# First adapter number read from DRAM, first weight chunk in two halves of k, ScalarE copies of the float32 chunks, a base block's sum later

## The chip, the cores and the metric

The kernel runs on one core of a Trainium2 chip. A core has TensorE (PE, matmuls), VectorE (DVE), ScalarE (ACT), GpSimd (POOL) and SyncE (SP), each with its own instruction queue, and 16 DMA engines that all queues share. The metric is the device time of one execution in microseconds (us), lower is better.

## The reference

For each of 8 batch elements, x is 256 tokens by 1024. A weight of 1024x1024 is picked by the element's adapter number, and the product goes through a feed-forward layer with a router over 15 entries that map to 8 experts of rank 16:

```python
w = weight[adapter_ids]
y = jnp.einsum('bsi,boi->bso', x, w)
base_out = jnp.einsum('btd,od->bto', y, base_W) + base_b
logits = jnp.einsum('btd,nd->btn', y, router_W) + router_b
probs = jax.nn.softmax(logits, axis=-1)
topk_p, topk_i = jax.lax.top_k(probs, E)
mapped = expert_map[topk_i]
onehot = (mapped[..., None] == jnp.arange(E)).astype(y.dtype)
w = jnp.einsum('btk,btke->bte', topk_p, onehot)
h = jnp.einsum('btd,erd->bter', y, A)
lora = jnp.einsum('bter,eor->bto', h * w[..., None], B) * 2.0
out = x + base_out + lora
```

All data is float32. The adapter numbers (`ids`) are an input in DRAM.

## The kernel before

Each element has two stages. **Stage 1** makes y in 8 chunks (`OC`) of 128 output columns, one weight chunk of 512 KB each, contracted over 8 blocks of k (`KC`). **Stage 2** multiplies y by the base weight, the router and the experts. To reach float32 accuracy at the rate of the fp32r type, every operand is split: ACT rounds it to fp32r (the `_hi` tile), DVE subtracts (`_lo`), and PE multiplies hi by hi, hi by lo and lo by hi. For element 0 alone the first two chunks (`F32_CHUNKS = 2`) are plain float32 matmuls on the raw weights (`stage1_float32`, L841 to L850), so that nothing has to be split ahead of them. Before them PE runs 13 warm-up matmuls (L962).

The base weight is used as seven blocks (Strassen-like): four loaded (r00, r01, r10, r11) and sums of them. `block_sum_1` (L703 to L706) makes r01 - r00 on DVE into the place of T1; ACT then rounds it (L483) and DVE makes its lo part (`t1_lo`, L722). `block_hi` (L431) and `block_lo` (L686) do the same for a loaded block: B00, B10 and B11 are numbers 1, 2 and 3 on the semaphore `blocks_lo_done`.

The order of the work is written by hand, one queue for each engine:

- SP loads the adapter numbers to SBUF (`ids_sb`, L269), waits for them, reads number 0 into a register (`adapter`, L272), issues the load of weight chunk 0 with it (L335, semaphore `w0_in`), then chunks 1 to 3 (L275), chunks 4 to 7 into early buffers (L339), the stage 2 weights, and later the residual and element 1.
- ACT issues the two halves of x of element 0 (`load_x0`, L373), rounds them (L460), rounds weight chunks 2 and 3 (`adapter_hi`) and 4 and 5 (`early_hi`), and goes through its loop over chunks (L465 to L479): `evacuate` copies the second half of a chunk's PSUM bank out, `make_y_hi` rounds a pair of chunks of y, and at chunk 6 it rounds block B00.
- DVE makes the lo parts of x (L768) and of the weights (L509, L514); in its loop over chunks (L771 to L786) it copies the two float32 chunks out of PSUM (L774), adds the halves of the others (`make_y_sum`, L527), makes y_lo of each pair (`make_y_lo`, L531), and at chunk 6 runs `block_sum_1`. Behind the loop come B00's and B10's lo parts, masks, routing, the two adds of the first products (`p1_added`), t1_lo, gates, B11's and b's lo parts, bias, `make_hwt_lo`, bias, x of element 1, `block_sum_2`, two weight chunks of element 1, `block_sum_4`, and the final adds (L787 to L822); then element 1 (L739).
- PE runs chunks 0 to 7, then `first_stage2` (L896 to L921), then elements 1 to 7. A chunk c waits for its weight's lo part and for `y_sum_done` of chunk c - 2 (L833, L834), since two PSUM banks alternate.

`make_y_lo` of a pair (j, j+4) is waited for by `plain` (L859): the last pair (3, 7) is used last, at PE's 13th k-step of it. `product(w_ps, ..., B10)` waits for `p1_added` 1 and `product(x_ps, ..., B10)` for `p1_added` 2 (L904, L906).

Of the kernel before, what the change touches and what calls it, by code (L numbers as in the profile page):

```python
# [36 lines left out]
def adaln_ffn_kernel(nc, xT, x, ids, wT, a_t, base_t, b_t, router_t, base_b, router_b, expert_map, out):  # L37
# [28 lines left out]
    with ExitStack() as ctx:  # L66
        def sem(name):
            return ctx.enter_context(nc.semaphore(name))
# [92 lines left out]

        ids_in = sem("ids_in")
        x0_in = [sem(f"x0_in{j}") for j in range(PIECES)]
        w0_in = sem("w0_in")
        x_in = [sem(f"x_in{h}") for h in range(2)]
        w_in = [sem(f"w_in{s}") for s in range(W_SLOTS)]
        early_in = [sem(f"early_in{i}") for i in range(OC - W_SLOTS)]
# [98 lines left out]

        @block.sync
        def _(sp):
            sp.dma_start(ids_sb[:, :], ids).then_inc(ids_in, 16)  # L269

            def adapter(b):
                return sp.value_load(ids_sb[0:1, bass.ds(b, 1)], min_val=0, max_val=wT.shape[0] - 1)  # L272

# [17 lines left out]
            def load_res(b, t, first=False):  # L291
                if not first:
                    if isinstance(b, int) and b == 1:
                        sp.wait_ge(stored_first[t], 16)
                    else:
                        sp.wait_ge(stored[t], 16 * (b - 1))
                sp.dma_start(res[:, t, :], x[b, t * P:(t + 1) * P, :] if first else
                             x[bass.ds(b, 1), t * P:(t + 1) * P, :].rearrange("b p d -> (b p) d")).then_inc(res_in[t], 16)
# [31 lines left out]
                        load_w(nxt, c)  # L330
                store_element(b, last)

            sp.wait_ge(ids_in, 16)
            id0 = adapter(0)
            sp.dma_start(w_raw[:, 0, :, :], wT[bass.ds(id0, 1), 0].rearrange("a p k o -> (a p) k o")).then_inc(w0_in, 16)  # L335
            for c in range(1, W_SLOTS):
                load_w(id0, c)
            for i in range(OC - W_SLOTS):
                sp.dma_start(early_raw[i][:, :, :], wT[bass.ds(id0, 1), ORDER[W_SLOTS + i]].rearrange("a p k o -> (a p) k o")).then_inc(early_in[i], 16)  # L339
            sp.dma_start(a_raw[:, :, :], a_t).then_inc(ar_in, 16)  # L340
            sp.dma_start(router_raw[:, :, :], router_t).then_inc(ar_in, 16)
            for h in range(2):
# [10 lines left out]
            sp.wait_ge(x0_lo_done, PIECES)  # L353
            for t in range(NT):
                load_res(0, t, first=True)
            id1 = adapter(1)
            for c in range(W_SLOTS):
                sp.wait_ge(y_ps_done, W_SLOTS + c + 1)
# [11 lines left out]
        def _(act):  # L370
# [12 lines left out]
            def adapter_hi(b, c):  # L383
                act.wait_ge(w_in[c % W_SLOTS], 16 * w_uses(b, c))
                nc.scalar.copy(w_hi[:, c % W_SLOTS, :, :], w_raw[:, c % W_SLOTS, :, :]).then_inc(w_hi_done, 1)  # L385

            def early_hi(c):

                act.wait_ge(early_in[c - W_SLOTS], 16)
                if c - W_SLOTS >= F32_CHUNKS:  # L390
                    act.wait_ge(y_ps_done, c - W_SLOTS + 1)
                nc.scalar.copy(w_hi[:, c % W_SLOTS, :, :], early_raw[c - W_SLOTS][:, :, :]).then_inc(w_hi_done, 1)
# [64 lines left out]
            for j in range(PIECES):  # L457
                k = slice(j * KP, (j + 1) * KP)
                act.wait_ge(x0_in[j], 16)
                nc.scalar.copy(x_split[:, k, 0, :], x0_raw[:, k, :]).then_inc(x0_hi_done, 1)  # L460
            for c in (2, 3):
                adapter_hi(0, c)
            for c in (4, 5):
                early_hi(c)
            for c in range(OC):  # L465
                if c >= F32_CHUNKS:
                    evacuate(0, c)
# [37 lines left out]
        def _(dve):  # L505
# [180 lines left out]
            def block_lo(n, block_of, src):  # L686

                dve.wait_ge(blocks_hi_done, n)
                nc.vector.tensor_tensor(st_lo[:, :, block_of, :], src, st_hi[:, :, block_of, :], ALU.subtract).then_inc(blocks_lo_done, 1)
# [13 lines left out]
            def block_sum_1():  # L703
                dve.wait_ge(r00_in, 16)
                dve.wait_ge(r01_in, 16)
                nc.vector.tensor_tensor(r_t1, r01, r00, ALU.subtract).then_inc(t_done, 1)  # L706
# [62 lines left out]
            for c in (2, 3):  # L769
                adapter_lo(0, c)  # L770
            for c in range(OC):  # L771
                if c < F32_CHUNKS:
                    dve.wait_ge(y_ps_done, c + 1)
                    nc.vector.tensor_copy(y_sum[:, ORDER[c], :], y_ps[:, c, 0:T]).then_inc(y_sum_done, 1)  # L774
                else:
                    make_y_sum(0, c)
                if c % 2:
                    make_y_lo(0, c // 2)
                if c < OC - W_SLOTS:
                    early_lo(c + W_SLOTS)  # L780
                if c == 4:
                    ar_lo()
                if c in (5, 6):
                    plain_lo(c - 5)
                if c == 6:
                    block_sum_1()  # L786
            block_lo(1, B00, r00)  # L787
            block_lo(2, B10, r10)
            masks()
            routing_logits(0)  # L790
# [39 lines left out]
        def _(pe):  # L830
# [10 lines left out]
            def stage1_float32(c):  # L841
                if c > 0:
                    pe.wait_ge(w_in[c], 16)
                for k in range(KC):
                    if c == 0 and k == 0:
                        pe.wait_ge(w0_in, 16)
                    if c == 0 and k % KP == 0:
                        pe.wait_ge(x0_in[k // KP], 16)
                    mm = nc.tensor.matmul(y_ps[:, c, 0:T], w_raw[:, c, k, :], x0_raw[:, k, :], start=(k == 0), stop=(k == KC - 1))  # L849
                mm.then_inc(y_ps_done, 1)  # L850
# [174 lines left out]
```

## Time and profile before

| | us |
|---|---|
| median of 3 runs | 403.43 (403.35 to 403.43) |
| profiled execution, its time | 404.47 |
| span of the profiled execution, first to last instruction | 402.7 |
| PE busy / DVE busy / ACT busy | 395.6 / 306.3 / 157.0 |

The span is what the profile's rows cover; 1.8 us of the profiled execution lie around it. Times in rows are microseconds from the span's start. PE is TensorE's matmuls, PEld its weight loads; "q1" is the DMA queue of SP, "q10" that of ACT, "q0" that of GpSimd. "idle before <-releaser" is how long the engine stood still ahead of the instruction, and what let it go.

### The profile page before, as it was taken

What the parts mean: (1) busy time and instruction counts of PE and PEld (TensorE: products, weight loads), DVE (VectorE), ACT (ScalarE), POOL (GpSimd) and SP (SyncE); (2) the same over time, 40 slices, a digit from 0 to 9 for tenths busy, and PEclk for the clock granted to TensorE, in tenths of its full rate; (3) what the DMA queues carried; (4) which work ended last, traced back from release to release, by engine and by line L of the source; (5) the groups of instructions that cost most, each with busy time, mean ns of one, the idle gap of its engine ahead of it and who ended that gap; (6) DMA issues with size and microseconds to landing.
All of it is one profiled execution on the core that took longest, in us unless ns stands there. A gap on an engine that the chain in (4) does not pass through costs nothing.

```text
span 402.7 us, 5975 instructions
## 1 busy us (share of the span) xinstructions
PE 395.6 (98%) x2102; PEld 348.9 (87%) x2102; DVE 306.3 (76%) x564; ACT 157.0 (39%) x223; POOL 2.0 (0%) x10
## 2 busy tenths in 40 slices
PE   6999999999999999999999999999999999999996
PEld 6888888888888888889888888888888898888885
DVE  2669999879978985688748896589856899468763
ACT  3658342663136421564025530265304642144300
POOL 0000001000000000000000000000000000000000
PEclk9999999999999999999999999999999999999999
DMA  7999106840268305573066520775026830464002
GB/s 287 396 392 399 48 0 208 278 144 0 104 221 300 105 0 174 190 260 104 0 208 226 213 81 0 260 256 200 13 68 245 292 125 0 138 225 161 2 0 104
DMA packets 25693, 64.71 MB, mean 161 GB/s; under 512 B 3410, under 2 KB 12626, under 8 KB 25682
## 3 DMA queue, kind: packets, MB, share of 16 engines
q1 hardware_dynamic: 25106, 62.47, 43.6%
q10 hardware_dynamic: 288, 1.05, 0.8%
q0 software_dynamic: 288, 1.05, 0.7%
q8 instruction: 6, 0.10, 0.1%
q14 instruction: 5, 0.04, 0.0%
HBM read 56.18 MB, written 8.39 MB: 160 GB/s over the span
## 4 chain that ended last, share of the span: by engine, by line
PE 86%; DVE 8%; ACT 2%; DMA 2%; issue 1%; SPq 0%; DVEq 0%
PE y_ps L836 26%; PE y_ps L838 13%; PE pl_ps L861 6%; PE x_ps L872 6%; PE x_ps L871 6%; PE x_ps L873 6%; PE s_ps L871 5%; PE s_ps L872 5%; PE s_ps L873 5%; PE pl_ps L862 3%; PE y_ps L849 2%; DMA w_raw<-in_wT 1%; DVE w_lo L509 1%; DVE res L618 1%; PE s_ps L886 1%; PE s_ps L888 1%
## 5 line engine op out<-in xcount | busy, mean ns | idle before, releaser
L836 PE MATMUL y_ps<-x_split,w_hi 128*128 128x512 f32 x496 | 173.4, 393 | 0.5 <-DVE y_sum L527 0.5
L838 PE MATMUL y_ps<-x_split,w_lo 128*128 128x256 f32 x496 | 138.9, 280 | 0.0
L836 PEld LDWEIGHTS y_ps<-x_split,w_hi 128*128 128x128 f32 x496 | 92.8, 187 | 22.0 <-DVE w_lo L509 1.1
L838 PEld LDWEIGHTS y_ps<-x_split,w_lo 128*128 128x128 f32 x496 | 93.7, 189 | 0.4
L385 ACT CAST w_hi<-w_raw 128x1024 fp32r<-128x1024 f32 x58 | 60.8, 1050 | 77.2 <-DMA w_raw<-in_wT 77.1
L509 DVE TENSOR_TENSOR w_lo<-w_raw,w_hi 128x1024 fp32r<-128x1024 f32 x58 | 70.9, 1224 | 19.5 <-ACT w_hi L385 17.9
L377 ACT COPY y_sum<-y_ps 128x256 f32<-128x256 f32 x62 | 23.0, 371 | 59.6 <-PE y_ps L838 59.6
L861 PE MATMUL pl_ps<-pl_split,y_hi 128*128 128x480 f32 x128 | 42.7, 383 | 0.0
L618 DVE TENSOR_TENSOR res<-x_ps,res 128x464 f32<-128x464 f32 (+1 forms) x30 | 19.5, 651 | 27.2 <-PE x_ps L888 15.1
L527 DVE TENSOR_TENSOR y_sum<-y_ps,y_sum 128x256 f32<-128x256 f32 x62 | 26.0, 420 | 15.2 <-ACT y_sum L377 15.0
L862 PE MATMUL pl_ps<-pl_split,y_lo 128*128 128x240 f32 x128 | 34.9, 273 | 0.0
L871 PE MATMUL s_ps<-st_hi,y_hi 128*128 128x464 f32 x80 | 30.5, 381 | 0.1
L618 DVE TENSOR_TENSOR res<-s_ps,res 128x512 f32<-128x512 f32 (+1 forms) x32 | 20.9, 675 | 11.9 <-PE s_ps L888 11.9
L872 PE MATMUL s_ps<-st_lo,y_hi 128*128 128x464 f32 x80 | 29.9, 373 | 0.0
L873 PE MATMUL s_ps<-st_hi,y_lo 128*128 128x464 f32 x80 | 29.7, 372 | 0.0
L381 ACT CAST y_hi<-y_sum 128x512 fp32r<-128x512 f32 x32 | 19.8, 620 | 23.7 <-DVE y_sum L527 23.1
L861 PEld LDWEIGHTS pl_ps<-pl_split,y_hi 128*128 128x128 f32 x128 | 24.1, 188 | 4.0
L531 DVE TENSOR_TENSOR y_lo<-y_sum,y_hi 128x512 fp32r<-128x512 f32 x32 | 22.1, 692 | 5.5 <-ACT y_hi L381 2.7
L862 PEld LDWEIGHTS pl_ps<-pl_split,y_lo 128*128 128x128 f32 x128 | 24.3, 190 | 0.0
L872 PE MATMUL x_ps<-st_lo,y_hi 128*128 128x464 f32 x64 | 23.9, 373 | 0.0
L871 PE MATMUL x_ps<-st_hi,y_hi 128*128 128x464 f32 x64 | 23.8, 373 | 0.0
L873 PE MATMUL x_ps<-st_hi,y_lo 128*128 128x464 f32 x64 | 23.8, 371 | 0.0
(111 smaller groups left out, 536.2 us busy)
## 6 DMA issues: line engine op xcount, KB each, us to landing
w_raw<-in_wT SPq DMA_DIRECT2D x60, 512.0 KB, 3.6
res<-in_x SPq DMA_DIRECT2D x16, 512.0 KB, 4.7
x_raw<-in_xT SPq DMA_DIRECT2D x14, 512.0 KB, 4.8
out<-res SPq DMA_DIRECT2D x13, 512.0 KB, 3.1
early_raw<-in_wT SPq DMA_DIRECT2D x4, 512.0 KB, 9.1
hi_raw<-in_base_t SPq DMA_DIRECT2D x2, 928.0 KB, 9.7
st_raw<-in_base_t SPq DMA_DIRECT2D x2, 928.0 KB, 10.8
x_raw<-in_xT ACTq DMA_DIRECT2D x2, 512.0 KB, 4.4
```

The costliest lines, as they stand in the source:

```text
L377: nc.scalar.copy(y_sum[:, ORDER[c], :], y_ps[:, c % 2, T:2 * T]).then_inc(y_part_done, 1)
L385: nc.scalar.copy(w_hi[:, c % W_SLOTS, :, :], w_raw[:, c % W_SLOTS, :, :]).then_inc(w_hi_done, 1)
L509: nc.vector.tensor_tensor(w_lo[:, s, :, :], w_raw[:, s, :, :], w_hi[:, s, :, :], ALU.subtract).then_inc(w_lo_done, 1)
L527: nc.vector.tensor_tensor(y_sum[:, o, :], y_ps[:, c % 2, 0:T], y_sum[:, o, :], ALU.add).then_inc(y_sum_done, 1)
L618: return nc.vector.tensor_tensor(res[:, t, cols], ps, res[:, t, cols], ALU.add)
L836: nc.tensor.matmul(y_ps[:, c % 2, :], w_hi[:, s, k, :], x_split[:, k, :, :].rearrange("p s t -> p (s t)"), start=(k == 0), stop=False)
L838: mm = nc.tensor.matmul(y_ps[:, c % 2, 0:T], w_lo[:, s, k, :], x_split[:, k, 0, :], start=False, stop=(k == KC - 1))
L861: nc.tensor.matmul(pl_ps[:, t, 0:2 * PL], hi, pl_split[:, k, :, :].rearrange("p s n -> p (s n)"), start=(k == 0), stop=False)
L862: mm = nc.tensor.matmul(pl_ps[:, t, 0:PL], lo, pl_split[:, k, 0, :], start=False, stop=(k == KC - 1))
L871: nc.tensor.matmul(dst, hi(j), st_hi[:, j, block_of, :], start=begins and j == 0, stop=False, skip_group_check=not begins)
L872: nc.tensor.matmul(dst, hi(j), st_lo[:, j, block_of, :], start=False, stop=False, skip_group_check=not begins)
L873: mm = nc.tensor.matmul(dst, lo(j), st_hi[:, j, block_of, :], start=False, stop=(j == KH - 1), skip_group_check=not begins)
```

## The change

Four edits, all in the work of element 0. SP reads adapter number 0 straight from DRAM into its register, and the DMA that brings the numbers to SBUF, for the later elements, moves behind the weight loads. The load of weight chunk 0 is split by k into two DMAs of 256 KB with a semaphore each, and chunk 0's matmuls wait for them one half at a time. The copies of the two float32 chunks out of PSUM move from DVE to ACT, between the roundings of weight chunks 2 to 5. On DVE, the lo part of block B00 moves from behind the chunk loop to chunk 6, where `block_sum_1` was, and `block_sum_1` moves behind the loop, ahead of B10's lo part.

```diff
-        w0_in = sem("w0_in")
+        w0_in = [sem(f"w0_in{j}") for j in range(PIECES)]
...
-            sp.dma_start(ids_sb[:, :], ids).then_inc(ids_in, 16)
-
...
-            sp.wait_ge(ids_in, 16)
-            id0 = adapter(0)
-            sp.dma_start(w_raw[:, 0, :, :], wT[bass.ds(id0, 1), 0].rearrange("a p k o -> (a p) k o")).then_inc(w0_in, 16)
+            id0 = sp.value_load(ids[0:1, 0:1], min_val=0, max_val=wT.shape[0] - 1)
+            for j in range(PIECES):
+                k = slice(j * KP, (j + 1) * KP)
+                sp.dma_start(w_raw[:, 0, k, :], wT[bass.ds(id0, 1), 0, :, k].rearrange("a p k o -> (a p) k o")).then_inc(w0_in[j], 16)
             for c in range(1, W_SLOTS):
                 load_w(id0, c)
             for i in range(OC - W_SLOTS):
...
+            sp.dma_start(ids_sb[:, :], ids).then_inc(ids_in, 16)
             sp.dma_start(a_raw[:, :, :], a_t).then_inc(ar_in, 16)
...
+            sp.wait_ge(ids_in, 16)
             id1 = adapter(1)
...
-            for c in (2, 3):
-                adapter_hi(0, c)
-            for c in (4, 5):
-                early_hi(c)
+            def evacuate_float32(c):
+                act.wait_ge(y_ps_done, c + 1)
+                nc.scalar.copy(y_sum[:, ORDER[c], :], y_ps[:, c, 0:T]).then_inc(y_sum_done, 1)
+
+            adapter_hi(0, 2)
+            evacuate_float32(0)
+            adapter_hi(0, 3)
+            early_hi(4)
+            evacuate_float32(1)
+            early_hi(5)
...
             for c in range(OC):
-                if c < F32_CHUNKS:
-                    dve.wait_ge(y_ps_done, c + 1)
-                    nc.vector.tensor_copy(y_sum[:, ORDER[c], :], y_ps[:, c, 0:T]).then_inc(y_sum_done, 1)
-                else:
+                if c >= F32_CHUNKS:
                     make_y_sum(0, c)
...
                 if c == 6:
-                    block_sum_1()
-            block_lo(1, B00, r00)
+                    block_lo(1, B00, r00)
+            block_sum_1()
             block_lo(2, B10, r10)
...
-                    if c == 0 and k == 0:
-                        pe.wait_ge(w0_in, 16)
                     if c == 0 and k % KP == 0:
+                        pe.wait_ge(w0_in[k // KP], 16)
                         pe.wait_ge(x0_in[k // KP], 16)
```

## Rows read from the trace of the kernel before

**Rows 1.** The page's 40 slices of the span: the granted clock in tenths.

```profile
PEclk9999999999999999999999999999999999999999
```

**Rows 2.** Waits of PE over the whole span: us in total, times, longest.

```profile
PE y_ps L849 <- DMA w_raw<-in_wT: 1.7, 1, 1.7
```

**Rows 3.** The chain of waits, first 8.5 us: start, us, what.

```profile
0.73 1.19 DMA ids_sb<-in_ids
1.94 0.46 SPq L272
2.89 5.57 DMA w_raw<-in_wT
```

**Rows 4.** Timeline of PE, 0 to 16 us.

```profile
1.50 5.33 PE L962 MATMUL s_ps<-ident 128*128 128x128 f32 x26 [1.50 <-POOL ident L978]
8.50 7.17 PE L849 MATMUL y_ps<-x_raw,w_raw 128*128 128x256 f32 x32 [1.67 <-DMA w_raw<-in_wT]
```

**Rows 5.** Line L272, all its instructions, then the one of 0 to 3 us.

```profile
L272 SPq TENSOR_LOAD <-ids_sb x15: 268/499/673, 1.9 to 352.6; - x15
...
L272 SPq TENSOR_LOAD <-ids_sb x1: 462/462/462, 1.9 to 1.9; - x1
```

**Rows 6.** DMA queues in 4.4 to 4.9 us, then in 4.9 to 5.4 us.

```profile
q10 hardware_dynamic: 51, 0.21, 101.5%
...
q1 hardware_dynamic: 18, 0.07, 75.2%
```

**Rows 7.** SP's timeline at 63.75, then DMA queues in 65.00-65.45, 65.45-65.90 us.

```profile
63.75 5.96 SPq L275 DMA_DIRECT2D w_raw<-in_wT  x3
...
q0 software_dynamic: 19, 0.08, 78.5%
...
q1 hardware_dynamic: 17, 0.07, 37.5%
```

**Rows 8.** Timeline of ACT, 4 to 14 us: start, us, engine, line.

```profile
4.59 1.04 ACT L460 CAST x_split<-x_raw 128x1024 fp32r<-128x1024 f32 x1 [1.69 <-DMA x_raw<-in_xT]
6.16 1.05 ACT L460 CAST x_split<-x_raw 128x1024 fp32r<-128x1024 f32 x1 [0.53 <-DMA x_raw<-in_xT]
11.00 1.04 ACT L385 CAST w_hi<-w_raw 128x1024 fp32r<-128x1024 f32 x1 [3.79 <-DMA w_raw<-in_wT]
12.27 1.04 ACT L385 CAST w_hi<-w_raw 128x1024 fp32r<-128x1024 f32 x1 [0.23 <-DMA w_raw<-in_wT]
```

**Rows 9.** Timeline of DVE, and one row of ACT at 30.27, 30 to 39 us.

```profile
30.27 1.75 ACT L432 CAST st_hi<-hi_raw 128x1856 fp32r<-128x1856 f32 x1
...
30.88 2.08 DVE L706 TENSOR_TENSOR hi_raw<-hi_raw 128x1856 f32<-128x1856 f32 x1
32.88 0.41 DVE L527 TENSOR_TENSOR y_sum<-y_ps,y_sum 128x256 f32<-128x256 f32 x1
33.98 0.69 DVE L531 TENSOR_TENSOR y_lo<-y_sum,y_hi 128x512 fp32r<-128x512 f32 x1 [0.69 <-ACT y_hi L381]
...
38.59 0.17 DVE L693 CAST map_f<-map_i 128x15 f32<-128x15 int32 x1
```

**Rows 10.** Timeline of PE at 36.12 and 42.49, and of DVE at 41.03.

```profile
36.12 0.38 PE L861 MATMUL pl_ps<-pl_split,y_hi 128*128 128x480 f32 x1
...
42.49 0.37 PE L871 MATMUL s_ps<-st_hi,y_hi 128*128 128x464 f32 x1
...
41.03 0.63 DVE L618 TENSOR_TENSOR res<-s_ps,res 128x464 f32<-128x464 f32 x1
```

**Rows 11.** Timeline of DVE, 50 to 70 us.

```profile
50.87 0.42 DVE L610 TENSOR_TENSOR hwt_lo<-s_ps,hwt_hi 128x256 fp32r<-128x256 f32 x1 [0.46 <-ACT hwt_hi L419]
...
64.35 1.22 DVE L509 TENSOR_TENSOR w_lo<-w_raw,w_hi 128x1024 fp32r<-128x1024 f32 x1 [0.20 <-DVE res L618]
...
68.96 0.42 DVE L527 TENSOR_TENSOR y_sum<-y_ps,y_sum 128x256 f32<-128x256 f32 x1
```

**Rows 12.** Timeline of PE, 69 to 73 us: chunks 3 and 4 of element 1.

```profile
69.52 0.47 PE L836 MATMUL y_ps<-x_split,w_hi 128*128 128x512 f32 x1 [0.34 <-DVE y_sum L527]
...
72.72 0.47 PE L836 MATMUL y_ps<-x_split,w_hi 128*128 128x512 f32 x1 [0.18 <-DVE y_sum L527]
```

## The prediction

> **What bounds the kernel now.** I read the page first: PE is busy 395.6 of 402.7 us and the granted clock is full in every slice [rows 1], so only time in which PE stands still can be won. The waits of PE come next: the one large wait behind the warm-up is 1.7 us for weight chunk 0 [rows 2]. The timeline of PE places it: the warm-up ends at 6.83, and chunk 0 begins at 8.50 [rows 4]. The chain of waits names what ends it: the adapter numbers' DMA (0.73 to 1.92), the register load (1.94 to 2.40), and the weight's DMA, issued at 2.89 and landed at 8.46 [rows 3]. Later PE stands still twice more, before chunks 3 and 4 of element 1, at 69.52 and 72.72, and both times DVE is the releaser [rows 12]. The timeline of DVE shows why: from 50.87 to 64.35 it works without a gap over 0.2 us, then through two weight chunks up to the y_sum of 68.96, on which chunk 3 waits [rows 11]. So the kernel has two tight places: its start, bound by a DMA, and 51 to 73 us, bound by DVE. What is won at the start must pass the second place to reach the end.
>
> Call X the time by which chunk 0 begins earlier. It can't exceed 8.50 - 6.83 = 1.67 us, since the warm-up stands ahead of it [rows 4].
>
> **Register load from DRAM.** Removed: the 1.19 us DMA and the wait for it. The SBUF load of 0.46 us becomes a DRAM load, a thing the trace doesn't have. Lower end: the fastest SBUF load, 0.27 us [rows 5]. Upper end: it takes as long as what it replaces, from 0.73 to 2.40, that is 1.67 us, since that also fetches the number from DRAM and then reads it; longer can't be excluded. I take the middle between this load's 0.46 from SBUF and 1.67, about 1.07 us, for the fetch is one trip to DRAM without descriptors. The register work between load and issue stays, 2.89 - 2.40 = 0.49 us. The first issue then falls at 0.73 + 1.07 + 0.49 = 2.29, which is 0.60 us earlier; the ends give 1.40 us earlier and none.
>
> The Trainium skill (Runtime: NRT & Kernel Launch, The ~15µs preamble/postamble breakdown) puts a load of a few registers from HBM at about 1.3 us, and a note on the same page has some 200 ns a register. By 1.3 us, an estimate from that page, the issue would be 0.37 us earlier and the total 0.2 us worse than my sum. No row here shows such a load.
>
> **Does an earlier issue make the data earlier?** The x halves are ahead of the weight. SP's queue moves no weight in 4.4 to 4.9 us, while ACT's queue fills the engines (101.5%); 18 packets of SP's queue start in 4.9 to 5.4, the first some 2.0 us behind the issue at 2.89 [rows 3, 6]. Either the engines serve x until it is through (then an earlier issue wins nothing), or a queue that joins a busy one needs about 2 us. The other place with two queues speaks for the second: SP's load issued at 63.75 has no packet until 65.45 and 17 in the 0.45 us after, while GpSimd's store is far from through and keeps moving [rows 7]; that is 1.7 us with no need to let the other finish. I take it that the start moves with the issue; sharing with the rest of x takes about 0.1 us of the 0.60 back, so 0.50. Ends: 0 and 1.3.
>
> **Two halves.** Weight chunks land one behind another every 12.27 - 11.00 = 1.27 us [rows 8], so half a chunk lands 0.63 us before the whole. The second half is needed 7.17 / 4 = 1.8 us behind PE's start, a half of a chunk [rows 4], so it is hidden, and so is the one more issue (about 0.4 us on SP's queue): chunk 2 lands at 11.00 and PE needs its split at 15.3. The Trainium skill (DMA: Bandwidth & Descriptors, Rules for kernel authors) says of two transfers to partition halves "Don't bother — they serialize". That is no loss here, because serial is what is wanted: the two x halves, issued together, were taken up at 4.59 and 6.16 [rows 8]. If instead both halves finished together, the 0.63 would be gone.
>
> X is then 0.50 + 0.63 = 1.13 us, and PE begins at 7.37. With the ends X is between 0.63 (less, if the register load takes over 1.67 us) and the cap of 1.67.
>
> **ScalarE's copies.** ACT does two copies of about 0.4 us instead of DVE. They lie in ACT's idle time (3.79 us before 11.00) or move early_hi(5), whose chunk PE needs 8 us later. PE's chunk 2 needs y_sum of chunk 0: ACT gives it behind w_hi of chunk 2, 11.00 + 1.04 + 0.4 = 12.4, well before the 15.3 - 1.1 = 14.2 at which PE comes. DVE's copy came only at 14.49 and would have held PE for about 0.7 us, so this edit is needed for X to survive; it is worth nothing by itself, for DVE has gaps up to chunk 7 and follows PE there.
>
> **Block sum later.** Here the order on DVE at the last chunk matters. I give times in PE's frame, as if X were 0, and subtract X at the end. Before: the sum r01 - r00 started at 30.88 without waiting for anything, y_sum of chunk 7 at 32.88, y_lo at 33.98 [rows 9]. After: B00's lo part must wait for ACT's rounding, 30.27 + 1.75 = 32.02 [rows 9]; it runs 32.05 to 34.05, so y_sum of chunk 7 begins at 34.05 and y_lo at 34.05 + (33.98 - 32.88) = 35.15. DVE is 1.17 us late; the rest of its queue is the same work (the sum and B00's lo part have changed places, both 2.0 us), so masks start at 38.59 + 1.17 = 39.76. Who waits?
> PE needs y_lo of the last pair at 36.12 [rows 10]; it is done at 35.15 + 0.69 = 35.84, hidden by 0.3 us.
> PE's product at 42.49 needs the add of 41.03 [rows 10]. The add now ends at 41.03 + 1.17 + 0.63 = 42.83, and PE resumes some 0.14 us after DVE's end (68.96 + 0.42 = 69.38, and PE at 69.52 [rows 11, 12]), so at 42.97: a new stall of 0.48 us. The next pair is covered by it.
> At 50.87 DVE had stood still for 0.46 us for ACT's hwt_hi [rows 11]. That gap now takes up part of the lateness: DVE reaches hwt_lo at 50.41 + 1.17 = 51.58, and ACT's part is ready at 51.3, so DVE is late by 51.58 - 50.87 = 0.71, say 0.7 us.
> From there DVE has no gap, so chunk 3 of element 1, which waits for DVE's y_sum of 68.96, comes at 69.52 + 0.7 in PE's frame, and chunk 4 at 72.72 + 0.7. The 0.48 us stall is inside this, not on top. Behind chunk 4 every wait is on work that follows PE, so the shift stays.
>
> **Sum.** The end moves by X - 0.7 = 1.13 - 0.7 = 0.43 us. Span 402.7 - 0.4 = 402.3 us, profiled execution 404.47 - 0.4 = 404.0, and the median, which is 1.04 us below the profiled execution, 403.43 - 0.4 = 403.0 us.
>
> **The rivals.**
> A, the start gains, the middle takes it all: the weight's packets can't start before x is through (rows 6 read the first way). X is 0.63 and the end comes 0.07 us later: 403.5 us. For it: x is issued 1.2 to 1.8 us ahead of the weight and fills the engines. Against: rows 7.
> B, the register load is quick (up to 0.5 us) and PE begins straight behind the warm-up: X 1.67, gain 0.97: 402.5 us. For it: SBUF loads of 0.27 [rows 5].
> C, the other side: the register load from DRAM waits behind x's traffic and takes about 2.6 us. The issue is then at 0.73 + 2.6 + 0.49 = 3.82, 0.93 us later; X = 0.63 - 0.93 = -0.3, and with the 0.7 us of the later block sum 404.4 us. It decides from X under 0.7, that is from a load over about 1.6 us; over 0.2% slower needs over 2.5 us.
> D, DVE's lateness is no bound: if something between 51 and 69 us waits for PE after all, the 0.7 doesn't arise and X comes through whole: 403.43 - 1.13 = 402.3 us. Against it: the row of 64.35 has a gap of 0.20 on DVE's own work [rows 11].
>
> **How the numbers follow.** 0.2% is 0.8 us, about what a measurement of this kernel can tell from no change. Forecast 0.45, A 0.2, B 0.15, C 0.08, D 0.12. Faster by over 0.8 us: half of B to all of it and most of D, together 0.22. Slower by over 0.8: most of C, 0.06. Within: 0.72. The range goes from B with a bit (402.4) to A with a register load near 2 us (403.43 + 0.7 - 0.3 = 403.8, and 0.1 for spread, 403.9).
>
> **What would show each step.** The first weight issue on SP near 2.3; the first packets of SP's queue near 4.3; chunk 0 on PE at about 7.4, with its second half unwaited; no PE gap before chunk 2; DVE's y_lo of the last pair about 1.2 us later against PE; a PE gap of about 0.5 us at the B10 product; gaps before chunks 3 and 4 of element 1 together about 0.7 us more than before. Wrong would be a later first issue, or an unchanged gap at chunk 3 with an early start.

## The result: 0.18% slower, and a profile of after that is shorter than that of before

The changed kernel takes 404.31 us (median of 13, 403.76 to 404.82) against 403.49 us for the kernel before, timed beside it (403.15 to 403.88): ratio 1.0018, 95% interval 1.0010 to 1.0026. I had forecast 403.0, and a range up to 403.9. The profiled execution of after took 404.08 us with a span of 402.3 us; the one of before took 404.47 and 402.7. So the two profiles say 0.4 us faster where the medians say 0.8 us slower. That is the first thing to explain: the profiled execution of before lies above all 13 timed ones. That the profile of after comes so close to the forecast for it (404.08 against 404.0) is luck, as the steps below show: two terms of the sum were wrong, and 0.2 us of the 0.4 arose behind the start of element 1, where nothing was changed.

The page of after, busy shares and the granted clock (full in every slice, as in [rows 1]):

```profile
PE 396.0 (98%) x2102; PEld 348.3 (87%) x2102; DVE 305.6 (76%) x562; ACT 157.7 (39%) x225; POOL 2.0 (0%) x10
...
PEclk9999999999999999999999999999999999999999
```

The waits of PE in after (us in total, times, longest). The wait for the weight is 0.4 us instead of the 1.7 of [rows 2]; new is the one for DVE's add (L625), at the B10 product:

```profile
PE s_ps L965 <- POOL ident L981: 1.5, 1, 1.5
PE y_ps L840 <- DVE y_sum L534: 0.6, 2, 0.4
PE y_ps L852 <- DMA w_raw<-in_wT: 0.4, 1, 0.4
PE s_ps L874 <- DVE res L625: 0.3, 1, 0.3
```

The chain of waits in after, first 11 us (start, us, what), which answers to [rows 3]. The register load from DRAM is two loads, 0.86 us for the pointer to the tensor and 2.11 us for the number itself (the rows of line L331 stand below); the first weight issue comes at 4.20, not at 2.29 as I had it and not at 2.89 as before. The chain then goes through the load of chunk 1, issued at 5.33 and landed at 10.75, for which PE stands:

```profile
0.71 0.86 SPq L331
1.59 2.11 SPq L331
3.74 0.17 SPq L331
4.20 0.40 SPq L334
4.79 0.35 SPq L334
5.33 5.42 DMA w_raw<-in_wT
10.79 0.48 PE y_ps L852
```

```profile
L331 SPq TENSOR_LOAD <-in_ids_ptr x1: 857/857/857, 0.7 to 0.7; - x1
L331 SPq TENSOR_LOAD <-in_ids x1: 2109/2109/2109, 1.6 to 1.6; - x1
```

And yet PE starts early. The timeline of PE in after, against [rows 4] and [rows 10]: chunk 0 at 6.94, the B10 product at 42.22 with a gap. Below them are four rows of DVE: B00's lo part, which waits 1.09 us for ACT's rounding, y_lo of the last pair, the add that the B10 product waits for, and hwt_lo, ahead of which DVE no longer stands still (0.46 us in [rows 11]):

```profile
6.94 7.58 PE L852 MATMUL y_ps<-x_raw,w_raw 128*128 128x256 f32 x32 [0.37 <-DMA w_raw<-in_wT]
...
42.22 0.45 PE L874 MATMUL s_ps<-st_hi,y_hi 128*128 128x464 f32 x1 [0.27 <-DVE res L625]
...
31.29 2.09 DVE L696 TENSOR_TENSOR st_lo<-hi_raw,st_hi 128x1856 fp32r<-128x1856 f32 x1 [1.09 <-ACT st_hi L433]
...
34.40 0.69 DVE L538 TENSOR_TENSOR y_lo<-y_sum,y_hi 128x512 fp32r<-128x512 f32 x1 [0.69 <-ACT y_hi L382]
...
41.45 0.63 DVE L625 TENSOR_TENSOR res<-s_ps,res 128x464 f32<-128x464 f32 x1
...
50.74 0.42 DVE L617 TENSOR_TENSOR hwt_lo<-s_ps,hwt_hi 128x256 fp32r<-128x256 f32 x1
```

Chunks 3 and 4 of element 1, against [rows 12]:

```profile
69.39 0.47 PE L840 MATMUL y_ps<-x_split,w_hi 128*128 128x512 f32 x1 [0.38 <-DVE y_sum L534]
72.58 0.47 PE L840 MATMUL y_ps<-x_split,w_hi 128*128 128x512 f32 x1 [0.18 <-DVE y_sum L534]
```

### The profile page after: what moved, and what is told of

It is laid out like the page before. It is cut to its first block, busy times and chain, and to the rows that moved or that the text cites. A ratio compares the mean times of both kernels' runs of the same rounds, so it can differ in the third digit from the quotient of the medians.

```text
span 402.3 us, 5980 instructions
## 1 busy us (share of the span) xinstructions
PE 396.0 (98%) x2102; PEld 348.3 (87%) x2102; DVE 305.6 (76%) x562; ACT 157.7 (39%) x225; POOL 2.0 (0%) x10
## 4 chain that ended last, share of the span: by engine, by line
PE 80%; DVE 13%; ACT 3%; DMA 1%; issue 1%; SPq 1%; DVEq 0%
PE y_ps L840 26%; PE y_ps L842 13%; PE pl_ps L864 5%; PE x_ps L875 5%; PE x_ps L874 5%; PE x_ps L876 5%; PE s_ps L874 4%; PE s_ps L875 4%; PE s_ps L876 4%; PE pl_ps L865 3%; DVE st_lo L696 2%; DVE res L625 1%; DMA w_raw<-in_wT 1%; DVE w_lo L516 1%; PE s_ps L889 1%
## 5 line engine op out<-in xcount | busy, mean ns | idle before, releaser
L625 DVE TENSOR_TENSOR res<-x_ps,res 128x464 f32<-128x464 f32 (+1 forms) x30 | 19.5, 651 | 27.5 <-PE x_ps L891 15.1
L534 DVE TENSOR_TENSOR y_sum<-y_ps,y_sum 128x256 f32<-128x256 f32 x62 | 26.1, 420 | 15.4 <-ACT y_sum L378 15.2
L625 DVE TENSOR_TENSOR res<-s_ps,res 128x512 f32<-128x512 f32 (+1 forms) x32 | 20.9, 675 | 11.9 <-PE s_ps L891 11.9
L382 ACT CAST y_hi<-y_sum 128x512 fp32r<-128x512 f32 x32 | 19.9, 621 | 23.4 <-DVE y_sum L534 23.4
L538 DVE TENSOR_TENSOR y_lo<-y_sum,y_hi 128x512 fp32r<-128x512 f32 x32 | 22.2, 692 | 5.4 <-ACT y_hi L382 2.6
```

Source lines behind the costliest of these rows:

```text
L534: nc.vector.tensor_tensor(y_sum[:, o, :], y_ps[:, c % 2, 0:T], y_sum[:, o, :], ALU.add).then_inc(y_sum_done, 1)
L625: return nc.vector.tensor_tensor(res[:, t, cols], ps, res[:, t, cols], ALU.add)
```

## The experiments

"before" in a time is always the kernel before, timed beside the run on the same chip. Chips and hours differ (its medians were 403.5 to 404.5 us), so only ratios are compared between groups. For each trace I read five landmarks from the timeline of PE; they carry most of what follows:

| trace | chunk 0 | stage 2 of el. 0 | element 1 | element 2 | element 3 | span |
|---|---|---|---|---|---|---|
| before | 8.50 | 32.16 | 60.55 | 110.40 | 158.78 | 402.7 |
| b_again (before) | 7.51 | 31.47 | 59.88 | 109.59 | 157.74 | 401.6 |
| before_3 (before) | 7.21 | 31.71 | 60.09 | 109.81 | 158.21 | 402.1 |
| after | 6.94 | 31.45 | 60.38 | 110.12 | 158.40 | 402.3 |
| after_again | 6.87 | 31.46 | 60.37 | 110.12 | 158.55 | 402.4 |
| after_3 | 6.81 | 31.43 | 60.33 | 110.26 | 158.78 | 402.6 |
| a_sbuf_ids | 7.21 | 31.18 | 60.10 | 109.88 | 159.16 | 403.0 |
| a_sum_early | 6.92 | 31.41 | 59.81 | 109.87 | 158.17 | 402.0 |
| a_whole_w0 | 7.48 | 31.45 | 60.34 | 110.76 | 160.12 | 404.0 |
| b_sum_late | 7.60 | 31.55 | 60.47 | 110.21 | 158.51 | 402.4 |
| b_dram_ids | 7.19 | 31.80 | 60.19 | 109.87 | 158.06 | 401.9 |
| b_halves_act | 7.24 | 31.24 | 59.65 | 109.47 | 157.75 | 401.6 |
| halves_act_2 (the same) | 7.21 | 30.84 | 59.23 | 109.10 | 157.66 | 401.5 |
| halves_act_3 (the same) | 7.44 | 31.40 | 59.80 | 109.68 | 158.11 | 402.0 |
| halves_only | 7.26 | 31.75 | 60.15 | 110.02 | 158.54 | 402.4 |
| act_only | 7.43 | 31.08 | 59.47 | 109.34 | 158.69 | 402.6 |
| sum_behind | 7.43 | 31.09 | 60.78 | 110.70 | 159.16 | 403.0 |
| x1_late | 6.19 | 30.96 | 59.35 | 109.22 | 157.78 | 401.7 |
| pool_sum2 | 7.31 | 30.96 | 61.96 | 112.18 | 160.41 | 404.3 |
| after_pool | 6.96 | 31.70 | 66.22 | 115.11 | 163.62 | 407.5 |

Where I give a stall of PE as a row's idle time, its start comes 0.16 us later still, since matmuls otherwise overlap their predecessors by that much.

Two things outside the edits move these landmarks. The 26 warm-up matmuls end anywhere from 6.09 to 7.42 us, and in three traces (after_3, halves_act_2, x1_late) the weight has landed 0.14 to 0.41 us before chunk 0 begins, so that there the warm-up sets its start. And PE's pace differs, which the next section shows; it is worth 0.3 us up to stage 2. What sets either isn't known.

From element 3 to the last matmul every trace takes 240.6 us. What is won or lost is decided before 160 us.

### How steady is the kernel before: b_again and before_3

No edit.

> The kernel before once more, for a second trace of it. Theory 1 (what the edits do to waits explains the loss): times within 0.1% of the kernel before, and a trace in which PE stands still at the same three places as in the first (about 0.5, 0.35 and 0.3 us at 69.5, 72.7 and 102.5). Theory 2 (PE's pace differs from execution to execution: a pair of an L836 and an L838 matmul took 347 ns in most stretches of the trace of before and 353 ns in 60 to 85 and 120 to 132 us): this trace is shorter than the first, about 401.7 us, with more pairs at 347 ns.

> The kernel before, third trace. If its usual start is the second trace's, weight chunk 0 lands at 7.4 to 7.7 and PE begins at 7.5; if both kinds are common, 8.5 is as likely. Element 1 begins at 59.9 in the first case, 60.5 in the second.

b_again: 403.67 us, before 403.67, ratio 1.0002 (0.9993 to 1.0011), profiled execution 403.43. before_3: 404.09, before 404.19, ratio 0.9994 (0.9978 to 1.0010). In b_again the chain of waits has the same steps as [rows 3], issued at 2.88, but the weight's DMA takes 4.59 us and not 5.57:

```profile
0.72 1.18 DMA ids_sb<-in_ids
1.92 0.46 SPq L272
...
2.88 4.59 DMA w_raw<-in_wT
7.51 1.56 PE y_ps L849 x6
```

So the same kernel starts PE at 8.50, 7.51 or 7.21 us, and the trace I predicted from had the latest start of the three. In before_3, where the start was earliest, PE then stood ahead of chunk 2 for DVE's copy of chunk 0, which came at 14.42, at its usual place:

```profile
14.99 0.47 PE L836 MATMUL y_ps<-x_split,w_hi 128*128 128x512 f32 x1 [0.60 <-DVE y_sum L774]
...
14.42 0.42 DVE L774 COPY y_sum<-y_ps 128x256 f32<-128x256 f32 x1
```

Theory 2, the pace, holds in part. A pair of an L836 and an L838 matmul takes 347 or 353 ns, in long stretches, in the same program. The timeline of PE at 20 us, before and then b_again, shows the next pair 0.34 and 0.35 us on; over the pairs of 15.4 to 31 us the means are 347 and 353 ns. Of the 20 traces nine have the first and eleven the second there. It is worth 0.3 us in 48 pairs:

```profile
20.03 0.39 PE L836 MATMUL y_ps<-x_split,w_hi 128*128 128x512 f32 x1
...
20.37 0.39 PE L836 MATMUL y_ps<-x_split,w_hi 128*128 128x512 f32 x1
```

```profile
20.17 0.40 PE L836 MATMUL y_ps<-x_split,w_hi 128*128 128x512 f32 x1
...
20.52 0.40 PE L836 MATMUL y_ps<-x_split,w_hi 128*128 128x512 f32 x1
```

### One edit undone: a_sbuf_ids, a_sum_early, a_whole_w0

a_sbuf_ids:

```diff
+            sp.dma_start(ids_sb[:, :], ids).then_inc(ids_in, 16)
...
-            id0 = sp.value_load(ids[0:1, 0:1], min_val=0, max_val=wT.shape[0] - 1)
+            sp.wait_ge(ids_in, 16)
+            id0 = adapter(0)
...
```

> The changed kernel with one edit undone: the adapter numbers come by DMA to SBUF first, as before, and the register is read from there. Theory D (the DRAM read costs): in the changed kernel the two register loads took 0.86 and 2.11 us, the first issue was at 4.20 instead of 2.89, and PE waited 0.3 us for chunk 1's weight, landed at 10.75. With the SBUF read the first issue is at 2.9 again, the first half lands no later than 7.0, chunk 1 lands near 9.7 without a wait, and the time falls by 0.3 us or more, to 404.0 or less. Theory S (the late block sum costs, the DRAM read doesn't): the time stays at 404.3, as DVE is late at hwt_lo whatever the start is.

Measured 403.80 us, before 403.67, ratio 1.0007 (0.9998 to 1.0016). The first issue is at 2.89 again, the first half lands at 7.17, chunk 1's weight at 9.23 without a wait. PE starts 0.27 us later than in after, is through with stage 1 0.27 us earlier (31.18), and element 1 begins 0.28 us earlier. The whole span is longer all the same, for this trace lost 1 us in element 2 (see act_only below); its execution took 404.83, 1.0 above the median.

a_sum_early:

```diff
-                    block_lo(1, B00, r00)
-            block_sum_1()
+                    block_sum_1()
+            block_lo(1, B00, r00)
```

> The changed kernel with one edit undone: on DVE the block sum is at chunk 6 again and B00's lo part behind the loop. Theory S (the late block sum costs 0.7 us at the DVE-bound stretch of 51 to 73 us): no PE gap at 42.2, DVE reaches hwt_lo without lateness, chunk 3 of element 1 begins about 0.6 us earlier than in the changed kernel, time 403.7. Theory D (the DRAM read is the whole loss): time stays at 404.3.

Measured 403.85 us, before 403.67, ratio 1.0008 (0.9999 to 1.0017). The gap at the B10 product is gone, and element 1 begins at 59.81, 0.57 us earlier than in after. Both theories were partly right: each of the two edits has a price.

a_whole_w0:

```diff
-            for j in range(PIECES):
-                k = slice(j * KP, (j + 1) * KP)
-                sp.dma_start(w_raw[:, 0, k, :], wT[bass.ds(id0, 1), 0, :, k].rearrange("a p k o -> (a p) k o")).then_inc(w0_in[j], 16)
+            sp.dma_start(w_raw[:, 0, :, :], wT[bass.ds(id0, 1), 0].rearrange("a p k o -> (a p) k o")).then_inc(w0_in, 16)
...
```

> The changed kernel with one edit undone: weight chunk 0 in one DMA. If halves win 0.63 us of landing time, chunk 0 begins at 7.6 to 8.5 here instead of 6.94. Theory P (the start is hidden by DVE's lateness): time moves by less than 0.3 us, since DVE in 51 to 73 us follows PE by about a half. Otherwise it moves by the whole 0.6 to 1.5 us, to 405 or more.

Measured 404.29 us, before 403.67, ratio 1.0020 (1.0011 to 1.0029). Chunk 0 begins at 7.48, earlier than I had expected for it, and the 0.54 us it loses against after are gone at 31.45, where both are the same: with one DMA less, chunk 1's weight lands at 9.82 and PE doesn't stand for it. In this one trace, with the number from DRAM, the halves bring nothing.

### One edit alone: b_sum_late, b_dram_ids, sum_behind

b_sum_late is the kernel before with the change's order of the block sum; b_dram_ids is the kernel before with the number from DRAM.

> The kernel before with one edit alone: B00's lo part at chunk 6, the block sum behind the loop. Theory S: PE stands 0.4 to 0.5 us at the B10 product near 42, element 1 begins 0.5 us later than in before, time 404.1 to 404.2 (0.5 us more). Theory N (DVE's slack takes it): no change.

Measured 404.90 us, before 404.51, ratio 1.0008 (0.9990 to 1.0027). The time doesn't resolve it, the trace does. The timeline of PE at the B10 product:

```profile
42.33 0.45 PE L871 MATMUL s_ps<-st_hi,y_hi 128*128 128x464 f32 x1 [0.27 <-DVE res L618]
```

The stretch from stage 2 of element 0 to element 1 takes 28.38 to 28.41 us in every trace without the late sum, sum_behind and the two with GpSimd apart, and 28.89 to 28.93 us in all six with it. The late sum costs 0.51 us.

> The kernel before with one edit alone: adapter number 0 from DRAM. The first issue moves from 2.89 to 4.2. Theory F (the engines serve x first, until 5.0 to 5.5, so the issue has slack): chunk 0 begins within 0.2 us of before's 7.5 to 8.5, but chunk 1's weight lands about 1.3 us behind chunk 0's as always, so no stall; time 403.7. Theory L (a later issue makes later data): chunk 0 begins up to 1.3 us later, 8.8, time 404.5 or more.

Measured 404.42 us, before 404.51, ratio 0.9996 (0.9980 to 1.0013). The loads took 0.85 and 1.87 us, the issue came at 3.96, and PE still began at 7.19, no later than in before. Theory F holds for the start; what it hadn't seen is that PE then stands 0.72 us for DVE's copy, as in before_3 (0.60), whose PE starts as early:

```profile
15.08 0.47 PE L835 MATMUL y_ps<-x_split,w_hi 128*128 128x512 f32 x1 [0.72 <-DVE y_sum L773]
```

sum_behind puts the sum behind the loop and leaves B00's lo part behind it:

```diff
-                if c == 6:
-                    block_sum_1()
+            block_sum_1()
             block_lo(1, B00, r00)
```

> The kernel before with block_sum_1 moved behind the loop and B00's lo part left behind it, so that DVE idles in the last chunk: DVE is late by the sum's whole 2.0 us less 0.1 instead of 1.17. Theory S (the stall at the B10 product is DVE's lateness less about 0.7 us of slack): PE stands 1.2 to 1.4 us near 42 instead of 0.43, time 405 or more (1.3 us above before). Rival (the stall comes from ACT's rounding of T1, which waits for the sum): stall 2.0 us or more, as ACT's copies all move.

Measured 405.15 us, before 404.19, ratio 1.0023 (1.0008 to 1.0038). The stall has the expected size but another place: PE stands at the B00 product, for B00's lo part, which now ends at 37.5, and there is no further stall at 42.

```profile
37.56 0.48 PE L870 MATMUL s_ps<-st_hi,y_hi 128*128 128x464 f32 x1 [1.03 <-DVE st_lo L689]
```

Stage 2 of element 0 takes 60.78 - 31.09 = 29.69 us, 1.29 more than without the move. So DVE's lateness in the last chunk does cost PE time, and the more of it the more. It also shows why the change, once it has put the sum behind the loop, moves B00's lo part to chunk 6.

### The other two edits: b_halves_act, halves_act_2, halves_act_3, halves_only, act_only

b_halves_act is the changed kernel with a_sbuf_ids' and a_sum_early's edits together: halves of chunk 0 and copies on ACT remain. It was run three times.

> The kernel before with the two edits that no trace speaks against: halves of weight chunk 0 and the copies on ACT; the number by SBUF and the block sum early. Expected by the theory that the DRAM read and the late sum are the two losses: PE starts at 7.2 as in the run with the SBUF number, no stall at chunk 1 or at 42, element 1 begins 0.3 to 0.5 us earlier than before, 403.3, faster than before by 0.1%. Rival (DVE binds the stretch of 51 to 73 us anyway): 403.7, as before.

> Halves of weight chunk 0 and the copies on ACT, without the DRAM read and the late sum, once more for a clean comparison. Its first trace had element 1 at 59.65, the second trace of before at 59.88. Theory (the two other edits are the loss, these two a gain of 0.2 to 0.3 us): 0.05 to 0.1% faster than before. Rival (nothing of the start reaches the end): ratio 1.000.

> Halves and ACT copies alone, third trace: element 1 at 59.2 to 59.7, median 0.2 to 0.5 us under before (ratio about 0.999).

Measured 403.47 us (before 404.51, ratio 0.9972, 0.9956 to 0.9987), 403.37 (404.04, 0.9976, 0.9956 to 0.9996) and 403.81 (404.19, 0.9978, 0.9964 to 0.9993). This version beats both kernels, by about 0.25% (1.0 us) against before. Element 1 begins at 59.56 on the mean of three traces, before's at 60.17, after's at 60.36. So the traces show 0.6 us of that 1.0.

> The kernel before with the halves of weight chunk 0 alone; the float32 chunks' copies stay on DVE. Theory C (DVE's copies at 14.5 hold chunk 2): PE starts at 7.2 to 7.4 and stands 0.6 to 0.8 us ahead of chunk 2, element 1 begins at 60.0 to 60.1, time as before. Rival: no stall, element 1 at 59.6, time 0.3 us under before.

> The kernel before with the copies of the float32 chunks on ACT alone. Theory C: no stall ahead of chunk 2 whenever PE starts; it starts at 7.2 to 7.5, so element 1 begins at 59.6 to 59.9, nearly as early as with halves too; time 0.3 to 0.6 us under before. Rival (the halves are the gain): as before.

halves_only: 404.26 us, before 404.25, ratio 0.9997 (0.9984 to 1.0010); PE starts at 7.26 and stands 0.28 us at 14.72 ahead of chunk 2 for DVE's copy, as theory C has it. act_only: 404.37, before 404.25, ratio 0.9997 (0.9982 to 1.0012), though its element 1 begins at 59.47, earlier than any other but halves_act_2 and x1_late. So at element 1 the copies alone bring nearly all that both edits do, but neither edit alone shows in the times, and what the halves add isn't shown. The trace of act_only lost the gain in element 2: the weight for chunk 5 landed late, ACT stood 1.97 us for it, and PE 0.28 and 0.18 us (ACT's row, then PE's two):

```profile
121.06 1.05 ACT L385 CAST w_hi<-w_raw 128x1024 fp32r<-128x1024 f32 x1 [1.97 <-DMA w_raw<-in_wT]
...
123.85 0.47 PE L839 MATMUL y_ps<-x_split,w_hi 128*128 128x512 f32 x1 [0.28 <-DVE y_sum L533]
127.05 0.47 PE L839 MATMUL y_ps<-x_split,w_hi 128*128 128x512 f32 x1 [0.18 <-DVE y_sum L533]
```

The same happened in a_sbuf_ids and a_whole_w0, so in 3 of 20 traces, with the late sum and without it. There stage 1 of element 2 takes 23.4 us and not 22.2 to 22.7. The profiled executions of a_sbuf_ids and a_whole_w0 lie 1.0 and 1.5 us above their medians, the one of act_only (404.38) lies on its median.

### The start: x1_late

b_halves_act, and x's second half issued by SP behind the first half of chunk 0:

```diff
-            for j in range(PIECES):
-                load_x0(j)
+            load_x0(0)
...
+                if j == 0:
+                    sp.dma_start(x0_raw[:, KP:KC, :], xT[0, :, KP:KC, :]).then_inc(x0_in[1], 16)
```

> Halves and copies on ACT, and x's second half issued by SP behind the first half of weight chunk 0. Theory F (the DMA engines serve x through, so the weight's first packets come at 4.9 whatever its issue): with only 512 KB of x ahead, the weight's first packets start at 3.9 to 4.2, its first half lands near 6.0, and PE begins straight behind the warm-up at 6.7 instead of 7.24; x's second half lands by 7.8, before 8.5. Theory J (a joining queue needs 2 us): first packets at 4.9 as before, chunk 0 at 7.2. Whole time by F 0.3 to 0.5 us less than without.

Measured 404.28 us, before 404.04, ratio 0.9996 (0.9977 to 1.0015). Theory F holds. The weight's issue is at 2.88 as ever, and now its packets start in 3.9 to 4.4 us (the DMA queues of that window):

```profile
q1 hardware_dynamic: 38, 0.08, 65.4%
```

against none until 4.9 with both halves of x ahead [rows 6]. In x1_late the first packet comes 1.03 us behind the issue. SP's loads need that on idle DMA engines, too: in the trace of before, x of element 2 is issued at 84.30, and its first packet comes 1.07 us later (0.97 to 1.15 us at the like places of five traces). So of the 2.0 us that [rows 6] show, 1.0 is the load's own, and 1.0 is spent behind x; the number from DRAM issues the load at 3.88 to 4.25 us, and its first packets come at 4.96 to 5.28, 1.03 to 1.08 us behind the issue and up to 0.35 us later than in the trace of before. By the same measure the 1.7 us of [rows 7] held 1.0 of the load's own.

PE begins at 6.19, straight behind the warm-up. But the second halves come later, and PE stands 0.95 us for the weight's:

```profile
6.19 1.89 PE L854 MATMUL y_ps<-x_raw,w_raw 128*128 128x256 f32 x8
9.03 3.29 PE L854 MATMUL y_ps<-x_raw,w_raw 128*128 128x256 f32 x14 [0.95 <-DMA w_raw<-in_wT]
```

Stage 2 begins at 30.96, among the 30.84 to 31.40 of the same kernel without it, and the time isn't better, as theory F had it, but 0.9 us above that kernel's (403.37 for halves_act_2, timed beside it), which the trace doesn't explain. I read it so that the start is bound by the bytes of the first 1.5 MB and their order only decides where PE waits for them; no run varies the bytes.

### DVE's stretch: pool_sum2, after_pool

block_sum_2 on GpSimd, in b_halves_act and in the changed kernel:

```diff
-            block_sum_2()
...
+            pool.wait_ge(r11_in, 16)
+            pool.wait_ge(t_done, 1)
+            nc.gpsimd.tensor_tensor(st_raw[:, :, T2, :], st_raw[:, :, T3, :], hi_raw[:, :, T2, :], ALU.subtract).then_inc(t_done, 1)
```

> The same kernel with block_sum_2 (2.0 us in DVE's gapless stretch from hwt_lo to chunk 2 of element 1) on GpSimd instead of DVE. Theory V (DVE's stretch of 51 to 73 us is what holds chunks 3 and 4): both PE gaps there, 0.50 and 0.34, go, and the time falls by 0.5 to 0.9 us to about 402.7. Rival D (something that waits for PE or a DMA sits in the stretch): the gaps stay above 0.3 us together and the time falls by less than 0.3.

> The changed kernel with block_sum_2 on GpSimd. By theory V the late sum's price at chunks 3 and 4 is gone, but the stall at the B10 product (0.43 us at 42.2) stays, since it comes before: element 1 begins at about 60.4 as in the changed kernel, the gaps at 69.4 and 72.6 go, time 403.4 to 403.6. If the stall at 42 were only part of DVE's lateness and made up later, the time would be that of the kernel without the late sum and block_sum_2 on GpSimd.

Measured 405.20 us (before 404.04, ratio 1.0020, 1.0003 to 1.0036) and 409.52 us (before 404.04, ratio 1.0122, 1.0093 to 1.0151). Both gaps at chunks 3 and 4 of element 1 are gone in both traces, as theory V says: stage 1 of element 1 takes 22.60 us against 23.3 to 24.1. But the time rose, for a price that neither theory had. Timelines of GpSimd and DVE in pool_sum2:

```profile
31.92 4.20 POOL L983 TENSOR_TENSOR st_raw<-st_raw,hi_raw 128x1856 f32<-128x1856 f32 x1 [30.38 <-DVE hi_raw L714]
...
32.79 3.88 DVE L539 TENSOR_TENSOR y_lo<-y_sum,y_hi 128x512 fp32r<-128x512 f32 x1 [0.69 <-ACT y_hi L383]
```

DVE's y_lo takes 3.88 us instead of the 0.69 of [rows 9], ends 0.55 us behind GpSimd's instruction (36.67 and 36.12), and PE stands 1.64 us for it. By the Trainium skill (SBUF — State Buffer, SBUF: two separate sides) the port pair that GpSimd and DVE share is locked by one instruction as a whole, for DVE where it reads two inputs from SBUF while GpSimd reads SBUF too; the trace agrees, with both instructions of that kind and 3.88 us instead of 0.69. In after_pool the same instruction lay at 37.56, and PE then stood 4.3 us:

```profile
37.56 5.88 POOL L982 TENSOR_TENSOR st_raw<-st_raw,hi_raw 128x1856 f32<-128x1856 f32 x1 [36.00 <-DVE hi_raw L713]
...
46.51 0.45 PE L868 MATMUL s_ps<-st_hi,y_hi 128*128 128x464 f32 x1 [4.31 <-DVE res L625]
```

### The changed kernel again: after_again, after_3

> The changed kernel once more, beside the others on one chip. Theory 1 (the loss lies ahead of element 2 and is the same in each execution): time 404.3, PE starts at 6.9, stands 0.3 us ahead of chunk 1 and 0.43 us at 42.2, and element 2 begins at 110.1, 0.5 us behind the second trace of before (109.59). Theory 2 (the loss is in element 2, where a late weight load cost 1.1 us in two of four traces): element 2's stage 1 takes 23.4 us instead of 22.3 in the slower executions.

> The changed kernel, third trace. Theory 1 (steady losses: late sum 0.5 to 0.6, DRAM read 0.15 to 0.3, halves and ACT copies gain 0.25): element 1 begins at 60.4, 0.5 us behind before, and the median is 0.5 to 0.7 us above before's. Theory 2 (late loads of element 2 make it): the trace's element 1 begins as in before, the median's distance comes with element 2's stage 1 above 23 us.

after_again: 404.14 us, before 404.51, ratio 0.9994 (0.9976 to 1.0011). after_3: 405.03, before 404.19, ratio 1.0013 (0.9997 to 1.0029). The kernel before scattered widely on those chips, so neither repeats the first result clearly. The traces are steady: PE begins at 6.81 to 6.94, waits for chunk 1, comes 0.42 to 0.43 us late to the B10 product, and is at element 1 at 60.33 to 60.38. The timeline of PE in after_3 has the wait for chunk 1 in a row of its own (in after it lies inside the 7.58 us of chunks 0 and 1):

```profile
10.75 3.72 PE L852 MATMUL y_ps<-x_raw,w_raw 128*128 128x256 f32 x16 [0.32 <-DMA w_raw<-in_wT]
```

Theory 1 holds up to element 1; theory 2 isn't seen in any trace of this kernel (22.4 to 22.6 us in element 2).

## Why the prediction was wrong, step by step

**The baseline of X.** This step failed first. I noted that the median was 1.04 us below the profiled execution and shifted the sum by it, as if the 1 us lay around the kernel. The part that mattered lay in the step I was costing: the weight's DMA took 5.57 us in that execution [rows 3] and 4.59 in the next. The room ahead of PE was 1.67 us in my trace, 1.26 in b_again and none in before_3, where the warm-up lasted until the weight landed. X was to be 1.13 us. Chunk 0 begins 1.56 us earlier than in my trace, 0.57 earlier than in b_again; but what PE keeps at its first stage 2 matmul is 0.71 against my trace, 31.78 - 31.45 = 0.33 us against the mean of before's three, and 31.47 - 31.45 = 0.02 against b_again.

**The register load from DRAM.** Forecast 1.07 us with an upper end of 1.67, measured 0.86 + 2.11 = 2.97 in after and 0.85 + 1.87 in b_dram_ids. Rival C had 2.6, from a wait behind x's traffic; that a DRAM number needs a pointer loaded first was in no step. Whether the second load, 1.80 to 2.12 us beside x's packets (which run from 1.75 us on), also waits for them, no run tells. Even the 1.3 us of the Trainium skill (Runtime: NRT & Kernel Launch, The ~15µs preamble/postamble breakdown) is under half of 2.97. Its price was small, because the next step failed too: 0.28 us (a_sbuf_ids against after at element 1), by way of chunk 1. In the kernel before, without halves, no price is shown: b_dram_ids is at element 1 at 60.19, before's three at 60.17 on the mean.

**Does an earlier issue make the data earlier.** Forecast yes, by [rows 7]; it is no. The issue moved from 2.89 to 4.20, its first packet only from 4.93 to 5.23, and chunk 0 began no later. The packets wait until x's are nearly through (x's last ones start at 5.4 to 5.9), x1_late shows that it is x they wait for, and an issue at 3.20 (before_3) has its first packet as early as one at 2.88, at 4.94. The first reading of [rows 6], rival A's, was right. The two errors cancelled at chunk 0, not at chunk 1, whose weight landed 0.3 us too late.

**Two halves.** The distance between the landings was right: 7.87 - 7.22 = 0.65 us in halves_only, forecast 0.63. But that isn't what the first half gains over a whole chunk. With the number from SBUF the first half lands at 6.80 to 7.40 us (six traces, mean 7.18), the whole chunk at 7.17 to 7.55 in five traces and at 8.46 in mine (mean of six 7.57): 0.4 us, and 0.2 without mine. Wrong, too, in that it adds to X by itself: with DVE's copies chunk 2 waits (halves_only), with the late issue chunk 1 does (after).

**ScalarE's copies.** Right: the 0.7 us stall ahead of chunk 2 that I had for DVE's copies shows in b_dram_ids (0.72) and before_3 (0.60). What I missed is that the kernel before sometimes has it already, so the edit has a worth of its own: act_only is at element 1 at 59.47, 0.7 us ahead of before's mean, where halves_only is at 60.15.

**Block sum later.** Right in mechanism and place, a little large. DVE's y_lo against PE's stage 2 is at 34.40 - 31.45 = 2.95 us, before at 33.98 - 32.16 = 1.82: 1.13 us late, forecast 1.17. At hwt_lo, in the same measure, DVE is (50.74 - 31.45) - (50.87 - 32.16) = 0.58 us late, forecast 0.71, and ACT's gap is used up as I had it. PE comes 0.27 + 0.16 = 0.43 us late to the B10 product, forecast 0.48. The price at chunk 3 of element 1 is 0.55 to 0.58 us, (69.39 - 31.45) - (69.52 - 32.16) = 0.58 against my trace and (68.86 - 31.47 = 37.39) 0.55 against b_again, forecast 0.7. Most of that is the stall at the B10 product; the gaps at chunks 3 and 4 grow by 0.04 us together. The last paragraph of the prediction named 0.7 us more there as a sign, which doesn't agree with its own step, where 0.48 of the 0.7 is that stall. Rival D is out: with 2 us taken from DVE's stretch both gaps vanish (pool_sum2).

**The sum.** Its form, X minus the block sum's price, holds. With measured terms it is 0.33 - 0.55 = -0.2 us, where I had 1.13 - 0.7 = +0.4. The traces agree (element 1 at 60.36 in after, 60.17 in before, means of three). The medians say 0.8 in the first comparison. Half of the distance between 0.2 and 0.8 comes from the mean, which holds my unusual trace. The only trace of before whose execution lies among the 13 timed ones of that comparison is b_again (403.43; the median is 403.49). Against it the profile of after is 0.65 us longer (404.08), and the landmarks say where: nothing at stage 2 of element 0 (31.47 and 31.45), 0.50 us at element 1, by the late sum, and 0.66 at element 3. The remaining 0.16 us up to element 3, and 0.17 between the profiles and the medians, stay open, and b_again is one trace, taken later. One trace in seven loses 1.1 us to a late weight in element 2, but none of after's three does, and what decides it wasn't found. The range was too narrow for a kernel whose executions differ by 1 us and whose trace I had once.

**The step that failed**, in one sentence: the 1.13 us of X were costed on a start that the usual execution doesn't have, with a register load of 1.07 us that took 2.97 and an earlier issue that would have won nothing, and against b_again X came out at 0.02 us, so that the late sum's 0.5 us stood alone.

**What can be said to be shown**: the late sum costs 0.5 us (six traces with it, eleven without, none between), and halves with ACT's copies gain 0.6 us at element 1 and 0.25% of the time. The DRAM read together with the halves costs about 0.3 us: with halves and ACT's copies, stage 2 of element 0 begins at 31.41 to 31.70 in the five traces with the number from DRAM (mean 31.49) and at 30.84 to 31.40 in the five with the number from SBUF and x issued as before (mean 31.12). That the sum of these is the whole measured 0.18% is not shown.

## What to carry to other kernels

Before costing a step at the start of a kernel, ask whether the profiled execution is a usual one: if it is 1 us off the median, that 1 us sits in some step, and it may be the one you mean to shorten. A step moved into an engine's idle gap is free only if it ends before the gap does; block_lo at chunk 6 waited 1.1 us for its input and pushed the one instruction that was due. And moving a load's issue earlier is worth nothing while the DMA engines still have an earlier megabyte to move; subtract the time that a load needs on idle engines (here 1.0 us) from its wait to see how much later it could be issued.

## What the runs showed of the hardware that I had not expected

- One int32 read from DRAM into a register of SP took two loads, 0.84 to 0.96 us and 1.80 to 2.12 us in seven traces; the same from SBUF took 0.46 us.
- A weight DMA on an otherwise silent queue, behind 1 MB of x on another, had its first packet at 4.88 to 4.96 us when issued at 2.88 to 3.20 us, and at 4.96 to 5.28 us when issued at 3.88 to 4.25 us. Behind half of x, issued at 2.88, it had it at 3.91 us. Some 1.0 us from issue to first packet was the least in all of them.
- The same 512 KB load of weight chunk 0, issued at 2.88 to 3.20 us in six traces, landed at 7.17 to 8.46 us, and not in the order of its issue.
- The matmul pair of 512 and 256 columns ran at 347 or 353 ns in stretches of tens of us with the granted clock at 1.00 of the upper level; no run tells what sets it.
- The 26 warm-up matmuls took 4.59 to 5.92 us from the same start of 1.50 us; no run tells what sets it.
- A DVE instruction of 0.69 us took 3.88 us beside a 4.20 us one of GpSimd.
